# Selective scans: state feeds on GpSimd from B rows repeated by DMA, decays in PSUM, and per-direction storage for a walk by chunks

## The chip, the cores and the metric

The kernel runs on one core of one Trainium2 chip. Its time is the device time of one execution in microseconds; given are three runs and their median. The engines are TensorE (PE; its weight loads are PEld), VectorE (DVE), ScalarE (ACT), GpSimd (POOL) and SyncE (SP, which issues DMAs).

## The reference

Four layers follow one another on an input of 4 x 192 x 56 x 56 in float32: a windowed attention with a mixer, a channel gate, a strip attention with a gated feed-forward block, and a selective scan over the image in four directions. Only the last one is touched. What it computes:

```python
xn = _ln_cf(x, ln_w, ln_b)
xz = jnp.einsum('dc,bchw->bdhw', in_proj_w, xn)
xc, z = jnp.split(xz, 2, axis=1)
xc = silu(depthwise_conv3x3(xc, conv_w) + conv_b)
x_hw = xc.reshape(Bsz, D, L)
x_wh = xc.transpose(0, 1, 3, 2).reshape(Bsz, D, L)
xs = jnp.stack([x_hw, x_wh, x_hw[..., ::-1], x_wh[..., ::-1]], axis=1)
x_dbl = jnp.einsum('kcd,bkdl->bkcl', x_proj_w, xs)
dts, Bv, Cv = jnp.split(x_dbl, [R, R + N], axis=2)          # R = 12, N = 4 states
dt = jax.nn.softplus(jnp.einsum('kdr,bkrl->bkdl', dt_proj_w, dts) + dt_proj_b[None, :, :, None])
A = -jnp.exp(A_log)
# per step:  h = exp(dt*A) * h + dt * B * u;   y = sum over states of h * C
ys = _selective_scan(xs, dt, A, Bv, Cv) + Ds[None, :, :, None] * xs
# the four directions are brought back to image order and added, then
# layernorm, * silu(z), output projection, + x
```

For each of 4 images, 192 channels, 4 directions (rows, columns, and both backwards) and 4 states a linear recurrence of 3136 steps is run.

## The kernel before, in words

The program is a row of stages, each with its own tiles and semaphores and a barrier behind it. Two are touched: `scan_inputs` (L2928) and `scans` (L3553). `scan_outputs` (L3310) follows and is not touched.

**scan_inputs** takes the image in 14 steps: two pairs of images, 7 chunks of 448 pixels (8 rows of 56). The 384 channels of an image pair are laid over 128 partitions x 3. For each step it normalizes (`square`, `root`, `normal`), projects (`project`), convolves with 27 operations on VectorE (`taps`), applies Silu (`inputs`) and makes two small products (`small`, PE L3120): the 48 rows of step sizes for all directions (`pD`) and the 32 rows of B and C (`pB`). ScalarE copies the first to `f_do` (L3196), the second in bf16 to `f_bo` (L3198); VectorE takes the remainder (L3291), ScalarE rounds it (L3202), VectorE takes the next one (L3295), so that B and C are stored as three bf16 parts, 96 rows in all. SP stores them in image order (`store_small` L3024, `store_steps` L3031). The ScalarE order in a step is square, maps, halo, root, small, middle, gates, inputs (L3217 to L3235).

**scans** walks 24 sections: 2 image pairs x 3 groups of 128 channels x 4 directions, in the order `ORDER = (0, 2, 1, 3)`. A section has 7 chunks, a chunk 2 units of two states each: 168 chunks, 336 units `j`. The order of work on every engine is written out by hand; semaphores join them.
- VectorE, per unit: `scan(j)` (two TENSOR_TENSOR_SCAN, L3884, in place in `h`, start value from the unit before last), `feed(j + 1)` (L3869: step input times B, to `h`), `read(j)` (L3891: `h` times C, to `prod`).
- TensorE: `spread` (L3705) multiplies a selector with the bf16 rows of B or C so that one row appears on all 128 partitions of PSUM, two states side by side in `pB` and in `pC` (one tile each); `add` (L3722) sums the products of all states into `pY` by an identity matrix, with the skip term or what another direction left; `step` (L3695) makes the step sizes of the next section from 12 rows.
- ScalarE: `parts` and `softened` (L3781 to L3801: Relu, Abs, Exp, Ln for softplus; the odd directions are written turned, with a stride), `decay` (L3811: exp(dt*A), to four SBUF tiles `s_da`), `evacuate` (L3824), and the turned copies `column` (L3773) and `column_x` (L3779, 3136 elements at once).
- GpSimd: `step_size` (L3907, Relu part plus Ln part) and `step_input` (L3918, dt times x) of the next section, one behind each unit's scans (L3930), and the store of the result (L3922).
- SP: x, B and C rows, and the 12 step rows of a chunk (L3665), four buffers.

The step sizes `dt` and step inputs `dtu` are whole-image tiles, two each, so a section's step sizes are all made before its first unit. All sections start from step rows, B and C rows in image order; the column directions are turned on ScalarE.

L1238 and L1239, in an earlier stage, load a row of 192 numbers onto 128 and 112 partitions by a DMA that repeats the row; they are read in the rows below.

```python
                u = dtu[s % 2][:, span(c)].rearrange("p (o n) -> p o n", o=1).broadcast_to([128, 2, CH])
                v.tensor_tensor(h[j % 4][:, :, :], u, pB[:, :, 0:CH], ALU.mult).then_inc(b_used, 1)
```

Of the kernel before, what the change touches and what calls it, by code (L numbers as in the profile page):

```python
# [16 lines left out]
N = H * W  # L17
# [79 lines left out]
SR = 4  # L97
RP = 10
# [2829 lines left out]
def scan_inputs(nc, x3, kept, xc, zs, dts, bcs):  # L2928
# [4 lines left out]
    with ExitStack() as ctx:  # L2933
# [28 lines left out]
        bo = [sb(f"f_bo{i}", [64, 3, CH], BF16) for i in range(NO)]  # L2962
        pA, pI, pD, pB = pt("f_pa", 3), pt("f_pi", 3), pt("f_pd"), pt("f_pb")
# [23 lines left out]
        dts_evac = sem("f_dts_evac")  # L2987
        hi_done = sem("f_hi_done")
# [4 lines left out]
        x_stored = [sem(f"f_x_stored{i}") for i in range(NO)]  # L2993
        block = ctx.enter_context(nc.Block())
# [18 lines left out]
        def _(sp):  # L3013
# [5 lines left out]
            def store_small(s):  # L3019
                q, o = s // NCH, s % NO  # L3020
                sp.wait_ge(lo_done, s + 1)
                sp.wait_ge(mid_done, s + 1)
                for i in range(2):
                    sp.dma_start(bcs[2 * q + i, :, span(s)].rearrange("(m r) n -> r m n", m=3),  # L3024
                                 bo[o][32 * i:32 * i + 32, :, :]).then_inc(x_stored[o], 16)

            def store_steps(s):
                q, o = s // NCH, s % NO
                sp.wait_ge(dts_evac, s + 1)
                for i in range(2):  # L3030
                    sp.dma_start(dts[2 * q + i, :, span(s)], do[o][64 * i:64 * i + NK, :]).then_inc(x_stored[o], 16)  # L3031
# [36 lines left out]
        def _(pe):  # L3068
# [51 lines left out]
            def small(s):  # L3120
# [10 lines left out]
                if s:  # L3131
                    pe.wait_ge(rest_done, s)
# [20 lines left out]
        def _(a):  # L3153
# [84 lines left out]
        def _(v):  # L3238
# [314 lines left out]
def scans(nc, xc, dts, bcs, dt_wT, dt_b, a_log, ds, sel, ident, ys):  # L3553

    with ExitStack() as ctx:
        sb = lambda name, shape, dt=F32: ctx.enter_context(nc.sbuf_tensor(name, shape, dt))  # L3560
# [16 lines left out]
        dt = [sb(f"s_dt{i}", [128, N]) for i in range(2)]  # L3577
        dtu = [sb(f"s_dtu{i}", [128, N]) for i in range(2)]
# [461 lines left out]
```

## Time and profile before

| | us |
|---|---|
| median of 3 runs | 5881.08 |
| lowest, highest | 5874.78, 5885.37 |
| profiled execution, span from first to last instruction | 5874.6 |
| profiled execution, its own time | not shown apart from the span |
| busy in the span: PE, DVE, ACT, POOL | 5234.5, 4111.9, 2823.1, 805.7 |
| DMA | 398.22 MB, mean 68 GB/s |

The span is one execution on the chip as the hardware profiler saw it. Busy time is the time in which an engine had an instruction under way; records of matmuls overlap, so a busy TensorE is not one at its peak. Starts are counted from the start of the span. A row of a timeline may hold several equal instructions (x2), and then gives their time together. "idle <-" names what ended the idle time ahead of an instruction.

### The profile page before, as it was taken

Reading aid. Unit: us, or ns where it says so; the run is one execution under the profiler, and the core shown is the slowest. Engines: PE = TensorE matmul, PEld = TensorE weight load, DVE = VectorE, ACT = ScalarE, POOL = GpSimd, SP = SyncE. Lnnn points to the kernel's source line nnn. Section 1 sums busy time; section 2 is a strip of 40 time slices with the busy share of each in tenths; the row PEclk is TensorE's granted clock in tenths of the full one; section 3 lists DMA queues with packets and bytes.
Section 4 is the critical chain, followed back from the end, with each engine's and each line's share of the span. In section 5 each row is a group of like instructions: output and inputs, shape, how many; then the busy total and the mean of one; then the engine's idle time right before and its main releaser. Section 6 shows DMA issues by size and latency. Waiting matters only on the chain. (4 is left out here: it accounts for less than half of the span.)

```text
span 5874.6 us, 85825 instructions
## 1 busy us (share of the span) xinstructions
PE 5234.5 (89%) x34692; PEld 2383.9 (41%) x34692; DVE 4111.9 (70%) x4899; ACT 2823.1 (48%) x3955; POOL 805.7 (14%) x826
## 2 busy tenths in 40 slices
PE   7799999999989989968869799989778888888879
PEld 2355555555544434445534333333233333333323
DVE  3477677776621122278878499959789999999963
ACT  1144444444432223245521455526587777867844
POOL 1000000000000011122243100000033333323300
PEclk9899999999999989989989899989889999999999
DMA  6522121221032223344433000013300000000034
GB/s 214 138 39 42 22 42 23 40 43 22 15 110 70 81 77 129 111 142 142 132 119 123 29 29 29 33 47 113 99 29 29 5 28 25 16 29 5 17 113 164
DMA packets 298982, 398.22 MB, mean 68 GB/s; under 512 B 143916, under 2 KB 281316, under 8 KB 295324
## 3 DMA queue, kind: packets, MB, share of 16 engines
q1 hardware_dynamic: 271452, 302.90, 17.6%
q0 software_dynamic: 16096, 73.39, 3.7%
q10 hardware_dynamic: 11040, 16.43, 0.9%
q8 instruction: 276, 4.52, 0.3%
q14 instruction: 118, 0.97, 0.1%
HBM read 226.16 MB, written 166.49 MB: 67 GB/s over the span
## 5 line engine op out<-in xcount | busy, mean ns | idle before, releaser
L3884 DVE TENSOR_TENSOR_SCAN s_h<-s_da,s_h 128x448 f32<-128x448 f32 x672 | 729.6, 1124 | 1.5 <-ACT s_da L3811 1.4
L3731 PE MATMUL s_py<-s_prod,s_idf 128*128 128x448 f32 x1344 | 586.6, 559 | 24.5 <-ACT s_ycol L3824 23.3
L622 PE MATMUL b_pc<-b_ca,b_wdm 128*113 128x392 f32 x1152 | 486.9, 520 | 31.9 <-DVE b_wdm L837 25.8
L3811 ACT ACTIVATE s_da<-s_dt,s_al 128x448 f32<-128x448 f32 x672 | 406.1, 658 | 198.3 <-DVE s_h L3884 147.6
L765 ACT ACTIVATE b_band<-b_psel 124x784 f32<-124x784 f32 x264 | 217.7, 825 | 427.5 <-PE b_psel L690 424.4
L622 PE MATMUL b_pc<-b_cb,b_wdm 128*113 128x392 f32 x960 | 403.0, 520 | 0.0
L3869 DVE TENSOR_TENSOR s_h<-s_dtu,s_pb 128x896 f32<-128x896 f32 x336 | 354.9, 1056 | 31.7 <-POOL s_dtu L3918 23.2
L3891 DVE TENSOR_TENSOR s_prod<-s_h,s_pc 128x896 f32<-128x896 f32 x336 | 360.8, 1074 | 0.1
L3907 POOL TENSOR_TENSOR s_dt<-s_dt,s_dtu 128x448 f32<-128x448 f32 x168 | 249.3, 1484 | 782.7 <-DVE s_h L3884 427.5
L2861 DVE SCALAR_TENSOR_TENSOR j_zc<-j_zt,kept_vec,j_zc 128x896 f32<-128x896 f32 x320 | 344.9, 1144 | 6.7 <-ACT j_zt L2803 6.4
L3731 PEld LDWEIGHTS s_py<-s_prod,s_idf 128*128 128x128 f32 x1344 | 249.2, 193 | 220.0 <-issue 167.3
L1059 DVE TENSOR_SCALAR b_band<-b_psel 124x784 f32<-124x784 f32 x104 | 101.3, 974 | 236.4 <-PE b_psel L690 235.3
L1374 ACT ACTIVATE c_hid<-c_ph,c_vec 128x448 f32<-128x448 f32 x168 | 106.2, 634 | 332.1 <-PE c_ph L1333 318.4
L749 ACT ACTIVATE b_at<-b_pbt 128x448 bf16<-128x448 bf16 x336 | 164.6, 543 | 168.7 <-PE b_pbt L668 168.7
L622 PEld LDWEIGHTS b_pc<-b_ca,b_wdm 128*113 128x113 f32 x1152 | 176.0, 178 | 137.0 <-issue 86.7
L2394 PE MATMUL e_pc<-e_at,e_diag 128*128 128x448 f32 x504 | 195.4, 549 | 37.7 <-ACT e_at L2421 37.6
L3791 ACT ACTIVATE s_dt<-s_pd,s_db 128x448 f32<-128x448 f32 x168 | 144.1, 858 | 141.7 <-PE s_pd L3702 141.7
L707 PE MATMUL b_po<-b_band,b_vt 124*32 124x112 f32 x5376 | 203.1, 275 | 1.2 <-ACT b_band L765 1.2
L3278 DVE SCALAR_TENSOR_TENSOR f_cv<-f_ct,kept_vec,f_cv 128x448 f32<-128x448 f32 x336 | 202.3, 672 | 0.0
L707 PEld LDWEIGHTS b_po<-b_band,b_vt 124*32 124x32 f32 x5376 | 153.2, 111 | 103.9 <-issue 103.2
L1267 POOL MEMSET kept_f_wt<- 128x192 f32 x1 | 0.3, 258 | 1416.1 <-POOLq L143 1416.1
L3702 PE MATMUL s_pd<-s_dtt,s_wd 12*128 12x448 f32 (+1 forms) x448 | 174.1, 589 | 20.6 <-DVE s_skip L3858 11.6
(726 smaller groups left out, 11252.0 us busy)
## 6 DMA issues: line engine op xcount, KB each, us to landing
b_qk<-mid_qkvp SPq DMA_DIRECT2D x96, 240.2 KB
d_vt<-mid_vd SPq DMA_DIRECT2D x200, 96.0 KB
d_qs<-mid_qd SPq DMA_DIRECT2D x20, 744.0 KB, 5.3
d_ks<-mid_kd SPq DMA_DIRECT2D x20, 744.0 KB, 7.7
b_v<-mid_qkvp SPq DMA_DIRECT2D x6, 1922.0 KB
mid_pout<-d_out POOLq DMA_DIRECT2D x20, 558.0 KB, 4.4
mid_qkvp<-a_out SPq DMA_DIRECT2D x42, 248.0 KB, 2.2
mid_qkvp<-a_out ACTq DMA_DIRECT2D x42, 248.0 KB, 2.1
```

Source lines behind the costliest of these rows:

```text
L622: mm = pe.matmul(pc[n % 2][0:113, 0:392], wdm[:, slot, p, 0:113], src, start=(w == STARTS[a]), stop=(w + 1 == STARTS[a + 1]))
L707: mm = pe.matmul(pO[32 * g:32 * g + 32, 112 * s:112 * s + 112], vt[:, 14 * hf + 4 * s + g + d, 32 * (h % 4):32 * (h % 4) + 32], band[hf][: ...
L765: a.activation(band[hf][:, 2 * dp:2 * dp + 2, c0:c0 + 2, :, :, :, :].rearrange("p d c t r a i -> p d (c t r a i)"), selection(h, x)[0:124, ...
L2394: mm = pe.matmul(pc[k % 2][t][:, 0:CH], diag[:, t, i, :], at[k % 4][:, t, dy:dy + 8, dx:dx + W], start=(i == 0), stop=(i == 8))
L2861: v.scalar_tensor_tensor(dst, src, gw[:, t, k:k + 1], dst, ALU.mult, ALU.add).then_inc(tap_done, 1)
L3278: v.scalar_tensor_tensor(dst, tap, cw[:, t, k:k + 1], dst, ALU.mult, ALU.add).then_inc(tap_done, 1)
L3731: mm = pe.matmul(y, idf[:, :], prod[j % 3][:, e, :], start=(pr == 0 and e == 0), stop=False)
L3811: last = a.activation(da[j % 4][:, e, :], dt[s % 2][:, span(c)], ACT.Exp, scale=al[:, u, n:n + 1])
L3869: v.tensor_tensor(h[j % 4][:, :, :], u, pB[:, :, 0:CH], ALU.mult).then_inc(b_used, 1)
L3884: v.tensor_tensor_scan(x, along(da[j % 4][:, e, :]), x, before_, ALU.mult, ALU.add).then_inc(scanned, 1)
L3891: v.tensor_tensor(prod[j % 3][:, :, :], h[j % 4][:, :, :], pC[:, :, 0:CH], ALU.mult).then_inc(c_used, 1)
L3907: p.tensor_tensor(put(dt[s % 2]), put(dt[s % 2]), put(dtu[s % 2]), ALU.add).then_inc(dt_ready, 1)
```

## The change

In `scans`:
- The feeds go from VectorE to GpSimd. B comes as float32 rows from DRAM: a DMA per chunk (two where a channel group spans two images) repeats the four rows of a direction over the partitions, into three tiles `s_bt`. TensorE spreads C alone; the B and C tiles in SBUF become one C tile, both images on its 96 partitions.
- The decays are written to PSUM: three tiles of one state each take the place of four SBUF tiles of two.
- Step rows, B rows and step sizes are stored in each direction's own order, so nothing in `parts` and `softened` is turned any more. `dt`, `dtu`, the Relu part and the Abs part are rings of chunks (4, 4, 6 and 3 pairs), and each chunk's step sizes are made six chunks ahead. Exp and Ln run on two chunks at once. x is turned by chunks.
- `h` has 6 tiles. VectorE's order per unit is scan(j), read(j - 1). The store of the result goes from GpSimd's queue to SP's.

In `scan_inputs`: ScalarE makes three more copies in each step (B and C in float32, and the step rows and the B and C rows once turned, into whole-image tiles); the remainder is taken from the float32 copy in SBUF, and SP stores B in float32 and C in three bf16 parts.

```diff
 scan_inputs
+        bf = [sb(f"f_bf{i}", [64, CH]) for i in range(NO)]
+        dcol = sb("f_dcol", [128, N])
+        bcol = sb("f_bcol", [64, N])
...
 store_small(s)
+                sp.wait_ge(b_evac, s + 1)
                 for i in range(2):
-                    sp.dma_start(bcs[2 * q + i, :, span(s)].rearrange("(m r) n -> r m n", m=3),
-                                 bo[o][32 * i:32 * i + 32, :, :]).then_inc(x_stored[o], 16)
+                    sp.dma_start(cs[2 * q + i, :, span(s)].rearrange("(m r) n -> r m n", m=3),
+                                 bo[o][32 * i + 16:32 * i + 32, :, :]).then_inc(x_stored[o], 16)
+                    sp.dma_start(brs[2 * q + i, s % NCH, 0:8, :], bf[o][32 * i:32 * i + 8, :]).then_inc(x_stored[o], 16)
+                if s % NCH == NCH - 1:
+                    for i in range(2):
+                        sp.dma_start(brs[2 * q + i, :, 8:16, :].rearrange("c r n -> r c n"),
+                                     bcol[32 * i + 8:32 * i + 16, :].rearrange("r (c n) -> r c n", c=NCH)).then_inc(col_stored, 16)
...
 small(s), ScalarE
+                if s == NCH:
+                    a.wait_ge(col_stored, 64)
-                a.activation(do[o][:, :], pD[:, 0, 0:CH], ACT.Copy).then_inc(dts_evac, 1)
+                a.activation(do[o][:, :], pD[:, 0, 0:CH], ACT.Copy)
+                a.activation(turned(dcol[:, :], s % NCH), img(pD[:, 0, 0:CH]), ACT.Copy).then_inc(dts_evac, 1)
                 a.wait_ge(bc_done, s + 1)
                 a.activation(bo[o][:, 0, :], pB[0:64, 0, 0:CH], ACT.Copy).then_inc(hi_done, 1)
+                a.activation(bf[o][:, :], pB[0:64, 0, 0:CH], ACT.Copy)
+                a.activation(turned(bcol[:, :], s % NCH), img(pB[0:64, 0, 0:CH]), ACT.Copy).then_inc(b_evac, 1)
...
 remainder(s)
+                v.wait_ge(b_evac, s + 1)
-                v.tensor_tensor(rest[:, :], pB[0:64, 0, 0:CH], bo[s % NO][:, 0, :], ALU.subtract).then_inc(rest_done, 1)
+                v.tensor_tensor(rest[:, :], bf[s % NO][:, :], bo[s % NO][:, 0, :], ALU.subtract).then_inc(rest_done, 1)
...
 scans
+        DR, UR, RR, ER, HR, BR = 4, 4, 6, 3, 6, 3
+        AHEAD = 6
+        bt = [sb(f"s_bt{i}", [128, NST, CH]) for i in range(BR)]
-        da = [sb(f"s_da{i}", [128, 2, CH]) for i in range(4)]
+        da = [pt(f"s_da{i}") for i in range(3)]
...
 SP
+            def load_b(t):
+                s, q, u, k, c = place(t)
+                if t >= BR:
+                    sp.wait_ge(fed, 2 * (t - BR + 1))
+                r = NST * (s % KD)
+                for i, d0, p0, m in PIECES[u]:
+                    rows = brs[2 * q + i, c, r:r + NST, :].rearrange("r n -> (r n)")
+                    sp.dma_start(bt[t % BR][p0:p0 + m, :, :].rearrange("p r n -> p (r n)"), rows.partition_broadcast(m)).then_inc(b_loaded[t % BR], 16)
...
+            load_step(0)
+            load_step(1)
+            load_x(0)
+            load_b(0)
+            load_step(2)
+            load_step(3)
+            load_c(0)
+            load_b(1)
+            load_b(2)
...
+            for t in range(NTS):
+                s, i = divmod(t, NCH)
+                if t + AHEAD + 2 < NTS:
+                    load_step(t + AHEAD + 2)
+                if t + BR < NTS:
+                    load_b(t + BR)
+                if s % KD == 1 and i == 0 and s // KD + 1 < NV:
+                    load_x(s // KD + 1)
+                if s % NSEC == NSEC - 2 and i == 0 and s // NSEC + 1 < NP2:
+                    load_c(s // NSEC + 1)
+                if s and s % KD == 0 and i == 3:
+                    store(s // KD - 1)
...
 TensorE
             for j in range(NJ):
+                t, pr = divmod(j, 2)
+                if pr == 0 and t + AHEAD < NTS:
+                    step(t + AHEAD)
                 if j + 1 < NJ:
+                    spread(j + 1)
+                add(j)
...
 ScalarE
+            def decay(m):
+                t, n = divmod(m, NST)
+                s, q, u, k, c = place(t)
+                if m >= 3:
+                    a.wait_ge(scanned, m - 2)
+                a.wait_ge(dt_ready, t + 1)
+                n += NST * k
+                a.activation(da[m % 3][:, 0, 0:CH], dt[t % DR][:, :], ACT.Exp, scale=al[:, u, n:n + 1]).then_inc(decay_ready, 1)
...
 VectorE
             for j in range(NJ):
-                if j == 0:
-                    feed(0)
                 scan(j)
-                if j + 1 < NJ:
-                    feed(j + 1)
-                read(j)
+                if j:
+                    read(j - 1)
+            read(NJ - 1)
...
 GpSimd
+            def feed(j):
+                t, pr = divmod(j, 2)
+                p.wait_ge(dtu_ready, t + 1)
+                p.wait_ge(b_loaded[t % BR], b_count(t))
+                if j >= HR:
+                    p.wait_ge(c_used, j - HR + 1)
+                    p.wait_ge(scanned, 2 * (j - HR + 3))
+                u = dtu[t % UR][:, :].rearrange("p (o n) -> p o n", o=1).broadcast_to([128, 2, CH])
+                p.tensor_tensor(h[j % HR][:, :, :], u, bt[t % BR][:, 2 * pr:2 * pr + 2, :], ALU.mult).then_inc(fed, 1)
...
             for j in range(NJ):
+                t, pr = divmod(j, 2)
+                if pr == 0 and t + 2 < NTS:
+                    step_size(t + 2)
+                if pr == 1 and t + 2 < NTS:
+                    step_input(t + 2)
+                if j + 2 < NJ:
+                    feed(j + 2)
```

## Rows read from the trace of the kernel before

**Rows 1.** Stretches: length, busy of PE, PEld, DVE, ACT, POOL, clock, DMA share, GB/s

```profile
3946.00:4256.00 310.00, 278.83 (x964) 92.62 (x962) 255.39 (x424) 195.34 (x248) 0.00 (x0) 0.96 0.31 102
4278.00:5660.00 1382.00, 1169.37 (x3903) 446.29 (x3904) 1368.74 (x1344) 1027.61 (x1517) 437.63 (x334) 0.98 0.05 18
```

**Rows 2.** Groups of instructions by line and shape, 4256 to 5665 us

```profile
L3884 DVE TENSOR_TENSOR_SCAN s_h<-s_da,s_h 128x448 f32<-128x448 f32 x672 | 729.6, 1124 | 1.5 <-ACT s_da L3811 1.4
...
L3731 PE MATMUL s_py<-s_prod,s_idf 128*128 128x448 f32 x1344 | 586.6, 559 | 24.5 <-ACT s_ycol L3824 23.3 <-DVE s_prod L3891 1.3
...
L3811 ACT ACTIVATE s_da<-s_dt,s_al 128x448 f32<-128x448 f32 x672 | 406.1, 658 | 198.3 <-DVE s_h L3884 147.6 <-POOL s_dt L3907 50.7
...
L3891 DVE TENSOR_TENSOR s_prod<-s_h,s_pc 128x896 f32<-128x896 f32 x336 | 360.8, 1074 | 0.1
...
L3869 DVE TENSOR_TENSOR s_h<-s_dtu,s_pb 128x896 f32<-128x896 f32 x336 | 354.9, 1056 | 31.7 <-POOL s_dtu L3918 23.2 <-PE s_pb L3719 8.6
...
L3907 POOL TENSOR_TENSOR s_dt<-s_dt,s_dtu 128x448 f32<-128x448 f32 x168 | 249.3, 1484 | 782.7 <-DVE s_h L3884 427.5 <-ACT s_dtu L3801 355.2
...
L3719 PE MATMUL s_pb<-s_bct,s_sel 96*128 96x448 bf16 x224 | 64.6, 371 | 35.0 <-DVE s_h L3869 33.8
...
L3779 ACT ACTIVATE s_xcol<-s_xt 128x3136 f32<-128x3136 f32 x6 | 36.5, 6090 | 0.0
...
L3719 PE MATMUL s_pb<-s_bct,s_sel 96*64 96x448 bf16 x224 | 31.8, 364 | 12.3 <-DVE s_h L3869 11.8
```

**Rows 3.** Timeline of VectorE, 4500 to 4514 us

```profile
4500.67 2.17 DVE L3884 TENSOR_TENSOR_SCAN s_h<-s_da,s_h 128x448 f32<-128x448 f32 x2
4502.77 1.05 DVE L3869 TENSOR_TENSOR s_h<-s_dtu,s_pb 128x896 f32<-128x896 f32 x1
4503.75 1.07 DVE L3891 TENSOR_TENSOR s_prod<-s_h,s_pc 128x896 f32<-128x896 f32 x1
4504.75 2.17 DVE L3884 TENSOR_TENSOR_SCAN s_h<-s_da,s_h 128x448 f32<-128x448 f32 x2
```

**Rows 4.** Timeline of GpSimd, 4500 to 4514 and at the start of the scans

```profile
4277.88 10.06 POOL L3918 TENSOR_TENSOR s_dtu<-s_dt,s_xt 128x448 f32<-128x448 f32 x7
...
4502.92 1.13 POOL L3907 TENSOR_TENSOR s_dt<-s_dt,s_dtu 128x448 f32<-128x448 f32 x1 [2.94 <-DVE s_h L3884]
4507.00 1.14 POOL L3918 TENSOR_TENSOR s_dtu<-s_dt,s_xt 128x448 f32<-128x448 f32 x1 [2.94 <-DVE s_h L3884]
```

**Rows 5.** Timeline of VectorE at the start and at the end of the scans

```profile
4279.04 1.09 DVE L3869 TENSOR_TENSOR s_h<-s_dtu,s_pb 128x896 f32<-128x896 f32 x1 [23.18 <-POOL s_dtu L3918]
4280.24 3.79 DVE L3884 TENSOR_TENSOR_SCAN s_h<-s_da,s_h 128x448 f32<-128x448 f32 x2
4283.95 1.05 DVE L3869 TENSOR_TENSOR s_h<-s_dtu,s_pb 128x896 f32<-128x896 f32 x1
...
5656.94 1.09 DVE L3891 TENSOR_TENSOR s_prod<-s_h,s_pc 128x896 f32<-128x896 f32 x1
```

**Rows 6.** Groups of GpSimd instructions by line and shape, whole span

```profile
L2351 POOL TENSOR_TENSOR e_rows<-e_pin 128x672 f32<-128x672 f32 x14 | 21.2, 1514 | 69.0 <-DMA e_pin<-mid_pout 68.2 <-POOL e_t L2372 0.7
...
L2361 POOL TENSOR_TENSOR e_s<-e_rows 128x21 f32<-128x21 f32 x14 | 3.5, 251 | 1.1
```

**Rows 7.** Groups of VectorE instructions by line and shape, whole span

```profile
L2903 DVE TENSOR_TENSOR j_z<-j_zc,j_z 128x896 f32<-128x896 f32 x13 | 14.1, 1085 | 0.0
```

**Rows 8.** DMA rate in 40 slices of 0.25 us, 1732 to 1742 us

```profile
GB/s 373 344 409 387 416 387 416 394 401 409 409 382 336 371 384 299 218 284 313 332 350 406 378 396 406 372 270 92 52 61 209 357 433 424 393 406 393 406 393 406
```

**Rows 9.** DMA rate in 40 slices of 0.4 us, 4254 to 4270 us

```profile
GB/s 160 85 103 99 354 63 220 157 470 408 439 408 345 428 502 361 329 314 235 235 267 172 267 267 298 204 258 208 126 65 45 54 22 18 0 0 0 0 0 0
```

**Rows 10.** Timelines of ScalarE and VectorE, 4090 to 4112 us (scan_inputs)

```profile
4093.20 0.53 ACT L3196 ACTIVATE f_do<-f_pd 128x448 f32<-128x448 f32 x1
4097.23 0.58 ACT L3202 ACTIVATE f_bo<-f_rest 64x448 bf16<-64x448 f32 x1 [2.65 <-DVE f_rest L3291]
...
4096.59 0.61 DVE L3291 TENSOR_TENSOR f_rest<-f_pb,f_bo 64x448 f32<-64x448 f32 x1
```

More of the change, by code:

```diff
@@ L3690, in _ @@
+            store(NV - 1)
+            for i in range(2):
+                sp.wait_ge(stored[i], 16 * NV // 2)
         @block.tensor
@@ L3720, in spread @@
-                mm.then_inc(done, 1)
+                        col = KD * NST * i + row
+                        mm = pe.matmul(pC[p0:p0 + m, e, 0:CH], selt[:, col:col + 1].broadcast_to([G, m]), src[:, span(c)], start=True, stop=True)
+                mm.then_inc(c_spread, 1)
             def add(j):
-                s, c, pr = place(j)
-                q, u, k = section(s)
-                t, v = j // 2, s // KD
+                t, pr = divmod(j, 2)
+                s, q, u, k, c = place(t)
+                v = s // KD
@@ L3778, in column_x @@
                     a.wait_ge(dtu_ready, NCH * KD * v)
-                a.activation(turned(xcol[:, :]), img(xt[v % 2][:, :]), ACT.Copy).then_inc(xcol_ready, 1)
-            def parts(s, c):
-                q, u, k = section(s)
-                n = NCH * s + c
-                if s >= 2:
-                    a.wait_ge(dtu_ready, NCH * (s - 1))
-                    a.wait_ge(decay_ready, UNITS * (s - 1))
-                    a.wait_ge(b_used, UNITS * (s - 1))
-                a.wait_ge(step_done, n + 1)
-                put = lambda t: turned(t[:, :])[:, 8 * c:8 * c + 8, :] if k % 2 else img(t[:, span(c)])
-                a.activation(put(dt[s % 2]), img(pD[n % 2][:, 0, 0:CH]), ACT.Relu, bias=db[:, u, k:k + 1])
-                a.activation(put(dtu[s % 2]), img(pD[n % 2][:, 0, 0:CH]), ACT.Abs, bias=db[:, u, k:k + 1]).then_inc(step_evac, 1)
@@ L3794, in softened, with parts @@
-            def softened(s, c):
-                k = ORDER[s % KD]
-                e = turned(dtu[s % 2][:, :])[:, 8 * c:8 * c + 8, :] if k % 2 else dtu[s % 2][:, span(c)]
-                n = NCH * s + c + 1
-                a.wait_ge(step_evac, n)
+                a.activation(img(xcol[:, span(c)]), turned(xt[v % 2][:, :])[:, 8 * c:8 * c + 8, :], ACT.Copy).then_inc(xcol_ready, 1)
+            def parts(t):
+                s, q, u, k, c = place(t)
+                if t >= RR:
+                    a.wait_ge(dt_ready, t - RR + 1)
+                a.wait_ge(step_done, t + 1)
+                a.activation(raw[t % RR][:, :], pD[:, 0, 0:CH], ACT.Relu, bias=db[:, u, k:k + 1])
+                a.activation(soft[t // 2 % ER][:, t % 2, :], pD[:, 0, 0:CH], ACT.Abs, bias=db[:, u, k:k + 1]).then_inc(step_evac, 1)
@@ L3824, in evacuate @@
                 a.activation(put, img(got) if k >= 2 else got, ACT.Copy).then_inc(y_evac, 1)
-            for c in range(NCH):
-                parts(0, c)
-                softened(0, c)
+            parts(0)
+            parts(1)
+            shrunk(0)
+            softened(0)
+            parts(2)
+            parts(3)
             a.wait_ge(a_ready, 2)
@@ L3939, in _, with step_size @@
-            store(3 * NP2 - 1)
-            for i in range(2):
-                p.wait_ge(stored[i], 16 * 3 * NP2 // 2)
+            def step_size(t):
+                p.wait_ge(log_taken, t // 2 + 1)
+                if t >= DR:
+                    p.wait_ge(decay_ready, NST * (t - DR + 1))
+                    p.wait_ge(dtu_ready, t - DR + 1)
+                p.tensor_tensor(dt[t % DR][:, :], raw[t % RR][:, :], soft[t // 2 % ER][:, t % 2, :], ALU.add).then_inc(dt_ready, 1)
+            def step_input(t):
+                s, q, u, k, c = place(t)
+                v = s // KD
+                p.wait_ge(dt_ready, t + 1)
+                if k == 1:
+                    p.wait_ge(xcol_ready, NCH * v + c + 1)
+                elif k == 3:
+                    p.wait_ge(xcol_ready, NCH * (v + 1))
+                else:
+                    p.wait_ge(x_loaded[v % 2], 16 * (v // 2 + 1))
+                if t >= UR:
+                    p.wait_ge(fed, 2 * (t - UR + 1))
+                x = xcol if k % 2 else xt[v % 2]
+                p.tensor_tensor(dtu[t % UR][:, :], dt[t % DR][:, :], x[:, span(c)], ALU.mult).then_inc(dtu_ready, 1)
@@ L3950, in network @@
+    return np.kron(np.eye(2), np.tile(np.eye(n), (3, 1))).astype(mybir.dt.np(BF16))
 def network(nc, a, s, out):
```

294 lines of the change are left out of this document (127 added, 167 removed).

## Prediction, made before the changed kernel was built or run

> **What bounds the kernel now.** I first read the table of busy times by stretch, for the two stages that the diff touches [rows 1]. In the scans, 4278 to 5660 us, VectorE is busy for 1368.7 of 1382.0 us, TensorE for 1169.4, ScalarE for 1027.6 and GpSimd for 437.6, with a DMA share of 0.05. So VectorE bounds this stage, a fourth of the whole span. Next come the groups by line [rows 2]: VectorE runs 672 scans, 336 feeds (L3869) and 336 reads (L3891), nothing else. Then the timeline of a steady stretch [rows 3]: two scans start at 4500.67, the feed at 4502.77, the read at 4503.75, the next scans at 4504.75. A unit (two states of one chunk) thus costs 2.10 + 0.98 + 1.00 = 4.08 us, without a gap, and a chunk, two units, 8.16 us. GpSimd's work starts at 4502.92, 0.08 us behind the scans' end (L3928 makes it wait for them), and lasts 1.13 us [rows 4].
>
> The whole walk, first feed to last read, is 4279.0 to 5658.0 [rows 5], 1379.0 us for 168 chunks (8.21 each).
>
> **The feeds.** 336 feeds leave VectorE. A unit is left with 2.10 + 1.00 = 3.10 us, a chunk with 6.20, the walk with 168 x 6.20 = 1042 us, if GpSimd delivers. On GpSimd a chunk now has one L3907 (1.13 us, always unit stride; its mean was 1484 ns because half of them were turned [rows 2]), one L3918 (1.14) and two feeds of 128x896. No such feed is in the trace. GpSimd's additions of two tensors took 251 ns for 21 elements and 1514 for 672 [rows 6], 1.94 ns an element; from 21 elements to the 448 of rows 4 it is (1.13 - 0.25)/427 = 2.06. So a feed costs between 1.13 + 448 x 0.00194 = 2.00 us and twice a 448, 2.26. I take 1.13 + 448 x 0.00206 = 2.05, since the 448 rows are the nearest in kind. Between instructions there is at most the 0.08 us seen behind a scan, and nothing where waits are met early; a feed has four waits. I take 0.04 each, ends 0 and 0.08. Sum: 1.13 + 1.14 + 2 x 2.05 + 4 x 0.04 = 6.53 us a chunk (ends 6.27 and 7.12). That is over 6.20: **GpSimd becomes the bound**, VectorE waits 0.33 us a chunk, and the walk is 168 x 6.53 = 1097.0. Less the 2.3 us of the first step size and input, which lie ahead of the first feed, plus the 4.3 of the last scans and reads behind the last feed, it is 1099.0, against 1379.0: **-280.0** (ends -324 and -181).
>
> The GPSIMD Engine Reference of the Trainium skill (3.1 and 4.1) speaks against such a move: elementwise work belongs on VectorE, GpSimd is about 2x slower with two inputs, 4497 ns for 2048 elements. By that page a feed would be estimated at 896/2048 x 4497 = 1967 ns and a chunk at 6.37 us, 27 us less than my sum.
>
> **The decays in PSUM.** The time of a scan from PSUM is not in the trace. A product with one operand in PSUM took 1056 ns (L3869, 896 elements [rows 2]), one of the same size with both in SBUF 1085 (L2903 [rows 7]), so PSUM does not cost VectorE more. I price a scan at the same 2.10 us a pair; it would have to rise by 0.16 us a pair before VectorE passes GpSimd. What the move is worth is read at the stage's start. The seven first step inputs run on GpSimd from 4277.88, back to back, in 10.06 us, 2.1 more than 7 x 1.14 [rows 4]; the first scan pair beside them takes 3.79 us instead of 2.17, while the next feed, with one operand in PSUM, takes its usual 1.05 [rows 5]. So a scan with both inputs in SBUF and GpSimd hold each other up, and a VectorE instruction with one input in PSUM does not. With the decays in PSUM all VectorE work of the stage is of the second kind: I put contention at zero, with the rival below for the case that it is not. The page SBUF — State Buffer of the Trainium skill ("Who interferes with whom") states this as a rule: at most one SBUF input, no contention; by it rival 3 has no time at all.
>
> **ScalarE.** Even with all its old work, 1027.6/168 = 6.12 us a chunk, it stays under 6.53. Its Relu, Abs, Exp and Ln lose their turned halves, and the last two are done for pairs of chunks, so it falls further. Four decays of 658 ns stay [rows 2]; three buffers let it run one to two scans ahead, and with that slack the largest single piece (a turned x chunk, 6090/7 = 870 ns) doesn't reach VectorE: 0.
>
> **TensorE.** The B spreads go: for the untransposed half they are 64.6 + 31.8/2 us (the 64-wide ones run in twos) [rows 2], for both halves about 161. There remain (1169.4 - 161)/168 = 6.0 us a chunk of records that overlap their followers, under 6.53: 0, though PE is the next one behind. Behind each read stand a C spread, the additions (559 ns a record) and at every other unit a step; the new order puts the spread first, so VectorE's next read, two scans later, finds it. Cover gone, PE would take over at 6.0, so it can cost nothing unless GpSimd is faster than I say. The granted clock was 0.98 (2.4 GHz level) at 85% busy; I see no reason for a fall.
>
> **B rows by DMA.** SP's queue gets one or two DMAs a chunk, 128 x 1792 x 4 B = 917 KB, 154 MB in all, in front of or behind the x loads, the stores and the step rows of the same queue. At 6.53 us a chunk that is 140 GB/s, in a stage that moved 18. The nearest row is the stretch with the repeated rows of L1238 and L1239: 0.25 us slices of 344 to 416 GB/s for ordinary loads, 270 at their start, then 92, 52, 61 and 209, back to 357 [rows 8]. Those four slices average 103, the five with the 270 are 137; the packets there are 768 B, against 7 KB now. So bounds are 103 and 400 GB/s, 8.9 and 2.3 us a chunk; I take 2.3 to 3.5, since these rows are long. Three buffers give two chunks, 13 us, from the feed that frees one to its next use; x and y (1568 KB, 4 us at 400) fit beside. Cost 0, cover GpSimd.
>
> **Start and stores.** The stage now waits for one chunk's chain, not seven. Before, the loads ran from 4254 at 0.4 us a slice and were over by 4268 [rows 9]; x, one B tile and the first steps, 1.57 + 0.92 + 0.2 = 2.7 MB, are through by 4264 if the same slices are added up, and landing and a step input (1.14) follow: first feed at 4266.5, not 4279.0: **-12.5** (0 to -15). GpSimd's store goes to SP, which waits for the evacuation of a chunk three back while B loads queue behind it; they have two chunks' cover: 0.
>
> **The stage before** (scan_inputs, 3946 to 4256). ScalarE gets three more copies in each of 14 steps: one plain (0.53 us, L3196 [rows 10]) and two turned; a turned 448 takes 870 ns inside one long copy [rows 2], and alone it pays its own start, so I take 1.05 to 1.1. In the trace ScalarE starts its small copies at 4093.20, VectorE the remainder at 4096.59, the middle copy at 4097.23 [rows 10]. Now the small copies end at 4093.2 + 0.5 + 1.05 + 0.5 + 0.5 + 1.1 = 4096.9: 0.3 us late, 14 times 4 us. Behind the last step 2.6 us of copies and four more DMA issues and landings lie open: 5. Sum **+9** (0 to +20).
>
> **Sum.** 5874.6 - 280.0 - 12.5 + 9 = 5591.1 us of span. The profiled execution's own time is not shown beside its span; the median of three runs is 6.5 over it, which I add: **5598 us**, 283 under 5881.
>
> **Rivals.**
> 1. VectorE stays the bound: a feed takes under 1.9 us on GpSimd. Then 6.20 a chunk, 55 less: 5543. For it: the slope of 1.94 and early waits; against it: 448 elements never took under 1.13. Chance 0.08.
> 2. The B rows bound: every descriptor reads the same 7 KB. At 131 GB/s a chunk takes 7.0 us, the walk 79 more: 5677; at the lowest 103 it is 8.9, and 5990. For it: the slices at 52 to 92; against it: the first of these rows passed at 270. Chance 0.10, most of it under 5850.
> 3. Slower than before: GpSimd still locks out the scans, because they write or take their start value in SBUF. Then 4.2 us of scans and 6.4 of GpSimd stand one behind the other, 10.6 us a chunk, 168 x (10.6 - 6.53) = 684 more: 6282. It decides from where 40% of the scan time ((8.21 - 6.53)/4.2) is so held. For it: 3.79 against 2.17; against it: the unhindered feed beside GpSimd. Chance 0.05.
> 4. Waits between the chunk rings (steps, soft pairs, decays) leave 0.3 to 1 us a chunk: 5650 to 5770. The trace of before has longer rings. Chance 0.09.
>
> The forecast has 0.68.
>
> **How the numbers follow.** Its own ends are 5598 - 44 = 5554 and 5598 + 99 + 11 = 5708. With rival 1 below and the nearer parts of 2 and 4 above, 5540 to 5725 leaves out two in ten. A measurement can tell 0.2%, 12 us. Slower: rival 3, and 0.02 of rival 2, 0.07. Same: 0.01. Faster: 0.92.
>
> **What would show it.** GpSimd over 95% busy in the walk with feeds of 2.0 to 2.1 us; VectorE waiting for GpSimd some 50 us in total; scan slots still 2.10 a pair; a walk of about 1100 us; DMA at 140 GB/s without GpSimd waiting for B tiles; the first feed near 4276 (9 us later start); scan_inputs 9 us longer. Wrong is: scans of 1.5 us or more beside feeds, GpSimd waiting on a DMA, or feeds over 2.3 us.

## The result and the profile after

| | us |
|---|---|
| after, median of 4 runs | 5559.86 (5545.01 to 5563.93) |
| before, beside it, median of 4 runs | 5881.15 (5874.78 to 5885.37) |
| ratio | 0.9446, 95% interval 0.9432 to 0.9461 |
| profiled execution after | span 5560.1, own time 5562.28 |

The kernel is 5.5% faster, 38 us under the forecast and inside its range. The page of the changed kernel, its costliest groups in the scans and the two B transfers (last two lines: KB each, us from issue to landing):

```profile
PE 5052.6 (91%) x33796; PEld 2334.1 (42%) x33796; DVE 3792.1 (68%) x4563; ACT 2672.0 (48%) x3851; POOL 1419.3 (26%) x1156
...
L3926 DVE TENSOR_TENSOR_SCAN s_h<-s_da,s_h 128x448 f32<-128x448 f32 x672 | 730.2, 1128 | 26.1 <-ACT s_da L3853 22.6
L3973 POOL TENSOR_TENSOR s_h<-s_dtu,s_bt 128x896 f32<-128x896 f32 x336 | 698.7, 2080 | 0.1
...
L3853 ACT ACTIVATE s_da<-s_dt,s_al 128x448 f32<-128x448 f32 x672 | 401.9, 637 | 13.0 <-DVE s_h L3926 12.9
...
L3933 DVE TENSOR_TENSOR s_prod<-s_h,s_pc 128x896 f32<-128x896 f32 x336 | 356.8, 1062 | 1.4 <-issue 0.7
...
L3948 POOL TENSOR_TENSOR s_dt<-s_raw,s_soft 128x448 f32<-128x448 f32 x168 | 189.7, 1129 | 348.5 <-ACT s_soft L3844 348.5
...
s_bt<-mid_brs SPq DMA_DIRECT2D x112, 896.0 KB, 4.4
s_bt<-mid_brs SPq DMA_DIRECT2D x112, 448.0 KB, 5.8
```

The scans cost what they cost before, 1128 ns against 1124, and so do the reads [rows 2]; the feeds have gone to GpSimd, at 2080 ns. Of GpSimd's 348.5 us of idle time 345.5 lie ahead of its first instruction in the stage; behind it there are 3. The busy times by stretch, to be held against [rows 1] (length, then PE, PEld, DVE, ACT, POOL, clock, DMA share, GB/s):

```profile
3946.00:4256.00 310.00, 284.71 (x980) 95.06 (x980) 256.04 (x420) 228.44 (x292) 0.00 (x0) 0.97 0.30 98
4280.00:5345.00 1065.00, 988.50 (x3016) 395.02 (x3017) 1047.10 (x1008) 858.19 (x1392) 1053.47 (x670) 0.99 0.54 166
```

In the scans GpSimd is busy for 98.9% and VectorE for 98.3%: two engines at their limit at once, and TensorE at 93% behind them. A steady stretch shows which of the two leads. First GpSimd's timeline, then VectorE's:

```profile
4698.56 2.08 POOL L3973 TENSOR_TENSOR s_h<-s_dtu,s_bt 128x896 f32<-128x896 f32 x1
4700.62 1.12 POOL L3963 TENSOR_TENSOR s_dtu<-s_dt,s_xt 128x448 f32<-128x448 f32 x1
4701.71 2.08 POOL L3973 TENSOR_TENSOR s_h<-s_dtu,s_bt 128x896 f32<-128x896 f32 x1
4703.76 1.14 POOL L3948 TENSOR_TENSOR s_dt<-s_raw,s_soft 128x448 f32<-128x448 f32 x1
4704.86 2.08 POOL L3973 TENSOR_TENSOR s_h<-s_dtu,s_bt 128x896 f32<-128x896 f32 x1
```

```profile
4700.69 2.19 DVE L3926 TENSOR_TENSOR_SCAN s_h<-s_da,s_h 128x448 f32<-128x448 f32 x2
4702.79 1.06 DVE L3933 TENSOR_TENSOR s_prod<-s_h,s_pc 128x896 f32<-128x896 f32 x1
4703.82 2.19 DVE L3926 TENSOR_TENSOR_SCAN s_h<-s_da,s_h 128x448 f32<-128x448 f32 x2
4705.93 1.06 DVE L3933 TENSOR_TENSOR s_prod<-s_h,s_pc 128x896 f32<-128x896 f32 x1
4706.98 2.19 DVE L3926 TENSOR_TENSOR_SCAN s_h<-s_da,s_h 128x448 f32<-128x448 f32 x2
```

From start to start GpSimd's four instructions are 2.06, 1.09, 2.05 and 1.10 us: a chunk takes 6.30, without a gap. A record is longer than its slot (2.08 for 2.05), because the next instruction's record begins before it ends. VectorE's units are 3.13 and 3.16 in turn, 6.29 a chunk, GpSimd's pace, and each scan pair starts 0.03 to 0.05 us behind the end of a feed (4700.64, 4703.79, 4706.94): GpSimd leads. VectorE by itself is faster. At the start of the walk, where feeds lie ready ahead of it, its unit is 2.11 + 0.97 = 3.08:

```profile
4296.27 2.19 DVE L3926 TENSOR_TENSOR_SCAN s_h<-s_da,s_h 128x448 f32<-128x448 f32 x2
4298.38 1.06 DVE L3933 TENSOR_TENSOR s_prod<-s_h,s_pc 128x896 f32<-128x896 f32 x1
4299.35 1.15 DVE L3926 TENSOR_TENSOR_SCAN s_h<-s_da,s_h 128x448 f32<-128x448 f32 x1
```

The last feeds and the last read:

```profile
5330.27 6.18 POOL L3973 TENSOR_TENSOR s_h<-s_dtu,s_bt 128x896 f32<-128x896 f32 x3
```

```profile
5342.43 1.09 DVE L3933 TENSOR_TENSOR s_prod<-s_h,s_pc 128x896 f32<-128x896 f32 x1 [0.70 <-PE s_pc L3771]
```

The first feed starts at 4279.66, so the walk, first feed to last read, is 5343.5 - 4279.7 = 1063.8 us, against 1379.0: -315.1. What lies ahead of the scans varies from one execution to the next: in the changed kernel and those below, the stage's first table load starts anywhere from 4249.4 to 4266.2, the first feed from 4263.4 to 4282.4. The walk doesn't hold that variation, and is the measure in all that follows. Two executions of the changed kernel gave walks of 1063.8 and 1061.1 us, so a difference of 3 us between single walks says nothing.

The start of the scans on ScalarE and GpSimd:

```profile
4263.38 1.28 ACT L3811 ACT_TABLE_LOAD   x1 [8.43 <-PEq L144]
...
4270.88 0.63 ACT L3833 ACTIVATE s_raw<-s_pd,s_db 128x448 f32<-128x448 f32 x1 [2.90 <-PE s_pd L3753]
...
4276.22 0.95 ACT L3844 ACTIVATE s_soft<-s_soft 128x896 f32<-128x896 f32 x1
```

```profile
4277.25 1.12 POOL L3948 TENSOR_TENSOR s_dt<-s_raw,s_soft 128x448 f32<-128x448 f32 x1 [345.54 <-ACT s_soft L3844]
4278.45 1.13 POOL L3963 TENSOR_TENSOR s_dtu<-s_dt,s_xt 128x448 f32<-128x448 f32 x1
4279.66 2.07 POOL L3973 TENSOR_TENSOR s_h<-s_dtu,s_bt 128x896 f32<-128x896 f32 x1
```

From the stage's table load to the first feed it is 16.3 us; before, from 4250.30 to 4279.04 [rows 5], it was 28.7.

The whole difference of the two profiled executions, 5874.6 - 5560.1 = 314.5 us, is made up so: walk -315.1, start -12.5, end of scan_inputs +5.6, and +7.4 that arise between 2154 and 3045 us, in stages that the change doesn't touch. What follows the walk takes 216.6 us in both.

### The profile page after: what moved, and what is told of

Read it like the earlier page. It is cut to its first block and busy times, and to the rows that moved or that the text cites. A ratio compares the mean times of both kernels' runs of the same rounds, so it can differ in the third digit from the quotient of the medians.

```text
span 5560.1 us, 84741 instructions
## 1 busy us (share of the span) xinstructions
PE 5052.6 (91%) x33796; PEld 2334.1 (42%) x33796; DVE 3792.1 (68%) x4563; ACT 2672.0 (48%) x3851; POOL 1419.3 (26%) x1156
## 5 line engine op out<-in xcount | busy, mean ns | idle before, releaser
L3926 DVE TENSOR_TENSOR_SCAN s_h<-s_da,s_h 128x448 f32<-128x448 f32 x672 | 730.2, 1128 | 26.1 <-ACT s_da L3853 22.6
L3973 POOL TENSOR_TENSOR s_h<-s_dtu,s_bt 128x896 f32<-128x896 f32 x336 | 698.7, 2080 | 0.1
L3783 PE MATMUL s_py<-s_prod,s_idf 128*128 128x448 f32 x1344 | 573.9, 549 | 0.0
L3948 POOL TENSOR_TENSOR s_dt<-s_raw,s_soft 128x448 f32<-128x448 f32 x168 | 189.7, 1129 | 348.5 <-ACT s_soft L3844 348.5
L3833 ACT ACTIVATE s_raw<-s_pd,s_db 128x448 f32<-128x448 f32 x168 | 106.4, 633 | 195.0 <-PE s_pd L3753 195.0
```

The source lines that it names most:

```text
L3783: mm = pe.matmul(y, idf[:, :], prod[j % 3][:, e, :], start=(pr == 0 and e == 0), stop=False)
L3926: v.tensor_tensor_scan(x, along(da[m % 3][:, 0, 0:CH]), x, before_, ALU.mult, ALU.add).then_inc(scanned, 1)
L3948: p.tensor_tensor(dt[t % DR][:, :], raw[t % RR][:, :], soft[t // 2 % ER][:, t % 2, :], ALU.add).then_inc(dt_ready, 1)
L3973: p.tensor_tensor(h[j % HR][:, :, :], u, bt[t % BR][:, 2 * pr:2 * pr + 2, :], ALU.mult).then_inc(fed, 1)
```

## The experiments

Each kernel is the changed one with the edit shown. The first four have one profiled run each, beside a run of before at 5884.93 us.

**Decays back in SBUF.** Do the PSUM decays keep GpSimd and the scans apart?

```diff
-        da = [pt(f"s_da{i}") for i in range(3)]
+        da = [sb(f"s_da{i}", [128, 1, CH]) for i in range(3)]
```

> The changed kernel with its three decay tiles in SBUF instead of PSUM, nothing else. Reference point: in the changed kernel the walk (first feed to last read) is 1064 us, 6.3 us a chunk. Theory (a scan with both inputs in SBUF and GpSimd's instructions hold each other up): GpSimd is never idle, so scans (4.2 us a chunk) and GpSimd's work (6.3) stand largely one behind the other: 8.5 to 10.5 us a chunk, walk 1430 to 1770 us, single scans up to 3 us. Rival (the decays' place does not matter, the unhindered first feed in the trace of before was luck): 6.3 us a chunk, walk within 10 us of 1064.

Measured: 6079.4 us, slower than before the change; the walk is 1587.1 us, as the theory had it. VectorE's timeline, then GpSimd's:

```profile
4701.68 3.81 DVE L3926 TENSOR_TENSOR_SCAN s_h<-s_da,s_h 128x448 f32<-128x448 f32 x2
4705.41 1.06 DVE L3933 TENSOR_TENSOR s_prod<-s_h,s_pc 128x896 f32<-128x896 f32 x1
4706.39 3.80 DVE L3926 TENSOR_TENSOR_SCAN s_h<-s_da,s_h 128x448 f32<-128x448 f32 x2
```

```profile
4702.61 1.92 POOL L3948 TENSOR_TENSOR s_dt<-s_raw,s_soft 128x448 f32<-128x448 f32 x1
4704.50 2.86 POOL L3973 TENSOR_TENSOR s_h<-s_dtu,s_bt 128x896 f32<-128x896 f32 x1
4707.33 1.92 POOL L3963 TENSOR_TENSOR s_dtu<-s_dt,s_xcol 128x448 f32<-128x448 f32 x1
```

A scan pair takes 3.73 us from start to start, not 2.10, and GpSimd's instructions are 0.8 us longer each; the read, with one operand in PSUM, keeps its 1.06. A unit takes 4.71 us. It isn't that scans from SBUF are slow by themselves: before the change their decays lay in SBUF too, and a scan took 1124 ns, with GpSimd mostly waiting. Only the decays changed place, and the walk is half a millisecond longer. The whole gain hangs on this one line.

**Feeds back on VectorE**, from the same SBUF B tiles, decays in PSUM. What does the rest of the change give without the move?

```diff
+            def feed(j):
...
+                v.tensor_tensor(h[j % HR][:, :, :], u, bt[t % BR][:, 2 * pr:2 * pr + 2, :], ALU.mult).then_inc(fed, 1)
             for j in range(NJ):
+                if j == 0:
+                    feed(0)
                 scan(j)
+                if j + 1 < NJ:
+                    feed(j + 1)
                 if j:
                     read(j - 1)
```

> The changed kernel with the feeds back on VectorE, B still from the tiles loaded by DMA, decays still in PSUM, rings and storage as changed. Theory (only the move of the feeds shortened the walk, the rest of the change is worth nothing there by itself): VectorE has 2.10 + 1.00 + 0.98 = 4.08 us a unit, walk 1371 us, plus what GpSimd's two instructions a chunk cost the feeds, which now have both inputs in SBUF: 1371 to 1500. Rival (the rings by chunk and the unit stride shorten the walk too): under 1320.

Measured: 5896.8 us, walk 1406.3. The groups of VectorE in the scans:

```profile
L3926 DVE TENSOR_TENSOR_SCAN s_h<-s_da,s_h 128x448 f32<-128x448 f32 x672 | 727.0, 1121 | 8.4 <-ACT s_da L3853 8.4
L3943 DVE TENSOR_TENSOR s_h<-s_dtu,s_bt 128x896 f32<-128x896 f32 x336 | 386.2, 1150 | 10.7 <-POOL s_dtu L3977 10.7
```

So without the move B rows by DMA, PSUM decays and chunk rings bring nothing to the walk; it is even 27 us longer than before. The feed group shows where: 386.2 us against 354.9 with B in PSUM [rows 2], 31 more. Most feeds take 1.05 or 1.07, and those beside a GpSimd addition up to 2.00. That is the hold of the experiment above again, now on a product whose operands are both in SBUF. The page SBUF — State Buffer of the Trainium skill ("Who interferes with whom") has it as a rule that a VectorE instruction with two inputs in SBUF contends with a GpSimd instruction that reads SBUF. Both runs agree, with scans of 1940 ns (median) beside GpSimd and feeds of up to 2.00 us. The walk's 315 us come with the feeds' place, given the PSUM decays. What the rest of the change does bring is the earlier start of the stage, 16.1 us from table load to first feed here too.

**A shorter read on VectorE.** Is VectorE a bound too? Left out: 64 of 448 columns of each product with C (the product tiles are set to zero once at the start).

```diff
-                v.tensor_tensor(prod[j % 3][:, :, :], h[j % HR][:, :, :], pC[:, :, 0:CH], ALU.mult).then_inc(c_used, 1)
+                v.tensor_tensor(prod[j % 3][:, :, 0:384], h[j % HR][:, :, 0:384], pC[:, :, 0:384], ALU.mult).then_inc(c_used, 1)
```

> The changed kernel with reads over 384 of 448 columns: the last 64 columns of each chunk's products are left out. VectorE has 0.27 us a chunk less, GpSimd the same. Theory (GpSimd bounds the walk at 6.29 us a chunk, VectorE with 6.20 is just behind): the walk stays at 1064 us within 5, and VectorE's idle time grows by 45 us. Rival (VectorE bounds): walk 45 us shorter, 1019.

Measured: 5553.45 us, walk 1061 us, what the unedited kernel has when it is run again (below). 336 reads are 0.13 us shorter, 44 us in all, and none of it is seen: GpSimd leads. VectorE's idle time ahead of its scans goes from 26.1 to 58.6 us, 32 of the 45 that were expected; the rest shows in no row.

**A shorter addition on GpSimd.** Left out: 224 of 448 columns of each step-size addition (those columns are set to a constant once at the start).

```diff
-                p.tensor_tensor(dt[t % DR][:, :], raw[t % RR][:, :], soft[t // 2 % ER][:, t % 2, :], ALU.add).then_inc(dt_ready, 1)
+                p.tensor_tensor(dt[t % DR][:, 0:224], raw[t % RR][:, 0:224], soft[t // 2 % ER][:, t % 2, 0:224], ALU.add).then_inc(dt_ready, 1)
```

> The changed kernel with the step size (Relu part plus Ln part) made by GpSimd for 224 of 448 columns, a constant in the others: half of that addition is left out. GpSimd has about 0.5 us a chunk less (5.8), VectorE the same 6.20. Theory (GpSimd bounds, VectorE is 0.1 behind): the walk gets 10 to 16 us shorter, 1048 to 1054, with VectorE busy over 99% and GpSimd idle 0.4 us a chunk. Rival (VectorE bounds already): walk 1064 within 3. Rival (both wait on something else, TensorE or the B loads): walk 1064 within 3 and VectorE still idle.

Measured: 5528.96 us, walk 1041.8. GpSimd was spared 0.47 us a chunk, 79 us, and the walk fell by 22. Over 1010 us of it the busy times are these (columns as in the stretches above):

```profile
4290.00:5300.00 1010.00, 963.47 (x2967) 385.24 (x2965) 1009.88 (x990) 839.70 (x1364) 959.46 (x658) 1.00 0.56 172
```

VectorE is idle for 0.1 us, and GpSimd is down to 95%: the bound has changed hands. The unit is 3.08 throughout, VectorE's own time as seen at the start of the changed kernel's walk, not the 3.10 that I had counted with: its read slot is 0.98, and the 1.03 and 1.05 in the changed kernel's steady stretch had 0.05 to 0.07 us of waiting in them that no row names. Hence a walk 6 us under the low end of what I expected.

**Both at once**, run last of all, beside a run of before at 5881.19 us. Its edit is the two above together.

> Left out of the computation: each read takes 384 of its 448 columns and each step-size addition 224 of 448. Alone, the shorter read left the walk of the scans at 1060.9 us (1063.8 in the changed kernel) and the shorter addition brought it to 1041.8. Theory (the two engines stand within a few per cent of each other, each with its own sum a chunk): GpSimd's chunk is 2 x 2.05 + 1.09 + some 0.6 = 5.8 us, VectorE's is 2 x (2.10 + 0.86) = 5.92 us, so the walk comes to 168 x 5.92 or a little more, 995 to 1012 us, with VectorE busy for over 98% of it. Rival (what is left of the stage is bound by something else, TensorE's queue of 5.6 to 6.0 us a chunk or the decays on ScalarE): it stays at 1025 to 1042 us.

Measured: 5507.03 us, walk 1011 us, 6.02 a chunk, at the upper end of the theory's range. Against the 1063.8 the read alone gave 3 us, the addition 22, both 53 (against the 1061.1 of the second execution: 0, 19 and 50). The stretch:

```profile
4290.00:5290.00 1000.00, 978.86 (x3009) 393.25 (x3008) 988.69 (x1006) 851.09 (x1383) 967.28 (x664) 0.99 0.56 175
```

VectorE is at 98.9% with units of 2.95 us in steady stretches. TensorE's records, which overlap, cover 97.9%; whether it would be the third bound wasn't tried.

The next four ran on one chip, beside 9 runs of before with the median 5882.81: the first with one run, the others with 4, 5 and 4.

**B rows loaded once.** Left out: the B tiles of all but the first three chunks, so the feeds multiply stale B rows. Are the loads hidden?

```diff
-            return 16 * sum(len(PIECES[place(i)[2]]) for i in range(t % BR, t + 1, BR))
+            return 16 * len(PIECES[place(t % BR)[2]])
...
-                if t + BR < NTS:
-                    load_b(t + BR)
```

> The changed kernel with the B tiles loaded for the first three chunks only and used for all 168: 151 MB of loads are left out (and with them the right B). Theory (the B loads are hidden behind GpSimd): walk 1064 us within 4, DMA share in the walk down from 0.54 to under 0.1. Rival (they hold the feeds or the scans up, by late tiles or by sharing SBUF): walk over 10 us shorter.

Measured: 5557.86 us, walk 1062.3 at 24 GB/s instead of 166. A difference of 1.5 us for some 150 MB (1065 us at 142 GB/s): they are hidden. In the changed kernel each load comes as a burst. The DMA rate in 40 slices of 1 us from 4700 us:

```profile
GB/s 380 36 0 0 93 337 423 108 0 0 0 237 437 287 0 0 0 115 409 375 63 0 0 108 387 375 90 18 0 50 344 366 371 301 131 0 151 409 375 35
```

Most slices that a load fills stand at 337 to 437 GB/s, and between two loads the queues are mostly idle. Over the same 40 us in slices of 0.25 us, as in [rows 8], low slices are still there near the start of a load, but one or two at a time (86 GB/s at 4705.0, 29 at 4717.75, 57 and 143 at 4736.5), where [rows 8] has four in a row.

**The changed kernel again**, as a control, with no edit.

> The changed kernel once more, as the control for the next two on the same chip: 5545 to 5565 us, walk 1064 us.

Measured: 5553.54 us (5544.73 to 5561.93), ratio 0.9441 (0.9428 to 0.9453), walk 1061.1.

**Softplus as ln(1 + exp(x)).** GpSimd's addition of the two parts goes, as ScalarE takes Exp straight from PSUM and Ln writes the step size; `dt` becomes a ring of three pairs.

```diff
-                a.activation(raw[t % RR][:, :], pD[:, 0, 0:CH], ACT.Relu, bias=db[:, u, k:k + 1])
-                a.activation(soft[t // 2 % ER][:, t % 2, :], pD[:, 0, 0:CH], ACT.Abs, bias=db[:, u, k:k + 1]).then_inc(step_evac, 1)
+                a.activation(soft[t // 2 % ER][:, t % 2, :], pD[:, 0, 0:CH], ACT.Exp, bias=db[:, u, k:k + 1]).then_inc(step_evac, 1)
...
-                a.activation(e, e, ACT.Exp, scale=-1.0).then_inc(exp_taken, 1)
...
-                a.activation(e, e, ACT.Ln, bias=1.0).then_inc(log_taken, 1)
+                a.activation(dt[g % ER][:, :, :], soft[g % ER][:, :, :], ACT.Ln, bias=1.0).then_inc(dt_ready, 2)
...
-                p.tensor_tensor(dt[t % DR][:, :], raw[t % RR][:, :], soft[t // 2 % ER][:, t % 2, :], ALU.add).then_inc(dt_ready, 1)
```

> The changed kernel with softplus as ln(1 + exp(x)) on ScalarE, written straight to the step sizes, in place of Relu, Abs, Exp, Ln there and an addition on GpSimd. GpSimd has 2 x 2.05 + 1.09 = 5.2 us a chunk left, ScalarE one instruction less. Theory (GpSimd bounds at 6.29, VectorE at 6.16 to 6.20 is next, TensorE at 5.6 behind it): walk 1040 to 1046 us, the kernel 15 to 25 us under the control, VectorE busy over 99% of the walk. Rival (TensorE or the loads come next before VectorE): walk over 1055 us, and VectorE idle.

Measured: 5528.61 us (5525.60 to 5543.34), ratio 0.9403 (0.9390 to 0.9416), walk 1044.7. The stretch:

```profile
4290.00:5300.00 1010.00, 963.04 (x2967) 385.45 (x2966) 1009.14 (x989) 694.40 (x1122) 857.79 (x491) 1.00 0.56 171
```

VectorE is the bound, at 99.9%, with GpSimd at 85% and ScalarE at 69%; walk and kernel (24.9 us under the control) are as the theory had them. The form has no guard for large x, where exp(x) overflows; the Relu and Abs form has one.

**The same with another start**: eight step-row buffers, six step rows issued ahead of the first B tile, the first two chunks' Ln taken one by one, and three decays ahead of the third chunk.

```diff
-SR = 4
+SR = 8
...
+            for t in range(2, 6):
+                load_step(t)
...
-            parts(0)
-            parts(1)
-            shrunk(0)
-            softened(0)
+            for t in range(2):
+                parts(t)
+                a.wait_ge(step_evac, t + 1)
+                a.activation(dt[0][:, t, :], soft[0][:, t, :], ACT.Ln, bias=1.0).then_inc(dt_ready, 1)
+                if t == 0:
+                    a.wait_ge(a_ready, 2)
+                    decay(0)
+                    decay(1)
+                    decay(2)
```

> The kernel of e_direct with another beginning of the scans: eight step-row buffers, six of them loaded ahead of the first B tile, softplus of the first two chunks one by one, and three decays made ahead of the later step sizes. In the changed kernel VectorE's first scan starts at 4284 and its second unit only at 4293, 14 us behind GpSimd's first feed. Theory (VectorE bounds now, so its own late start counts in full): 8 to 14 us under e_direct. Rival (the lag is made up behind the rings of six units, as GpSimd runs ahead): within 3 us of e_direct.

Measured: 5527.06 us (5521.24 to 5529.88), ratio 0.9394 (0.9382 to 0.9407), walk 1034.0, 10.7 shorter than without the new start. VectorE's start, in the changed kernel and then in this one:

```profile
4284.19 2.07 DVE L3926 TENSOR_TENSOR_SCAN s_h<-s_da,s_h 128x448 f32<-128x448 f32 x2 [15.28 <-ACT s_da L3853]
4293.31 2.07 DVE L3926 TENSOR_TENSOR_SCAN s_h<-s_da,s_h 128x448 f32<-128x448 f32 x2 [7.05 <-ACT s_da L3853]
```

```profile
4280.13 4.10 DVE L3921 TENSOR_TENSOR_SCAN s_h<-s_da,s_h 128x448 f32<-128x448 f32 x4 [12.62 <-POOL s_h L3961]
```

The 7 us wait ahead of the second unit is gone. But part of the walk's gain is a later first feed: it waits for its B tile, behind the extra step rows, until 16.0 us after the stage's table load, against 14.0 in the kernel without the new start. Counted from the table load to the last read the stage takes 1050.0 against 1058.7 us, 8.7 less. In the kernel's time, of which the expectation spoke, the two medians are only 1.5 us apart, with overlapping intervals. In the two profiled executions the stages ahead of the scans took 12.6 us longer with the new start (table load at 4262.1 against 4249.4), in which the edit changes nothing; that covers the stage's gain there. The gain stands in one profiled execution each, and whether it reaches the total isn't settled.

## Why the prediction was right, and where it was 38 us high

**The feeds.** Right in mechanism: GpSimd took the bound and VectorE stood just behind. The term was mis-sized, "6.53 us a chunk" against 6.30. Its feed of 2.05 was right, as the slot (its record is 2.08). The two additions have slots of 1.09 and 1.10, not 1.13 and 1.14, which is 0.08: I used the length of lone records as if it were their slot. And "0.04 each" for the waits between the four instructions, 0.16 a chunk, was nothing: the timeline has no gap. From the first feed's start to the last feed's end it is 1056.8 us against the 1094.7 of the working, and from there to the last read's end 7.1 instead of 4.3: the last three feeds have no addition between them and follow at 2.06 us each, faster than VectorE's units of 3.08, so the last scans start 2.1 us behind the last feed's end, and the last read waits another 0.7 for its C. Together the walk is 35.2 us under the forecast. By the figure of the Trainium skill (GPSIMD Engine Reference, 3.1) the estimates were 1967 ns a feed and 6.37 us a chunk. That was nearer for the chunk, but by luck: its feed is too short (2.05 us as a slot, 2080 ns as a record), and this made up for the same additions and waits that I had too long.

**VectorE's wait.** "0.33 us a chunk, some 50 us in total" was wrong with it. The rows name 26.1 us ahead of the scans, nearly all of it at the start (15.3 + 7.1) and for ScalarE's decays, not for GpSimd. The waiting for GpSimd is the difference between units of 3.08 at the start and 3.13 and 3.16 later, 0.13 us a chunk. The two engines were 2% apart rather than 5, so little was missing for rival 1 (VectorE stays the bound). With GpSimd eased it is what happens: VectorE alone bounds the versions without the addition, at 6.16 us a chunk in its slots, where the rival had 6.20.

**The decays in PSUM.** Right: pairs kept their 2.10 beside a GpSimd that is never idle, and without PSUM the hold is there. Rival 3 had the hold come from the scans' write and start value in SBUF. The changed kernel has both there, and its scans aren't held; it is the second input in SBUF that does it. The rival's price for a held walk, 10.6 us a chunk, is not far from that of the run with the decays in SBUF, 1587.1/168 = 9.4: each side was held for part of the other's instruction, not for all.

**ScalarE and TensorE at zero.** Right: 858 and 989 us of 1065, with no wait for them in a steady row. The 22.6 us that VectorE waits for ScalarE's first decays lie at the start, while GpSimd goes on with its feeds. TensorE's records were put at 6.0 us a chunk and cover 989/1065 of 6.30, 5.85.

**B rows.** Right: hidden, by the experiment. The mean is 166 GB/s: 917 KB in 6.30 us are 146, where I had 140 for a longer chunk, and the other transfers of the stage come on top. Rival 2 falls (its far end, at 8.9 us a chunk, adds up to 5996 and not to 5990). Low slices come with these loads too, but too few to matter; what makes them wasn't tried.

**Start.** -12.5 forecast, -12.5 measured (28.74 to 16.28), but not by the wait that I had worked out, the loads' landing with a step input behind it. The first step size waits for ScalarE (345.54 <-ACT s_soft), and step size and step input lie between that and the first feed. The loads would have allowed a start about 2.3 us sooner: without the addition the feed waits for its B tile and starts 14.0 us behind the table load, not 16.3. That the number fits to 0.1 us is luck.

**scan_inputs.** +9 forecast, +5.6 measured. The tail, from the last normalization to the next stage's table load, went from 53.8 to 59.5 us, +5.6 where 5 was put. The "0.3 us late, 14 times" didn't come: the step takes 20.63 us in both kernels, though ScalarE is busy for 33 us more in the stretch (228.4 against 195.3 [rows 1]). These are the new ones:

```profile
4101.07 1.01 ACT L3219 ACTIVATE f_dcol<-f_pd 128x448 f32<-128x448 f32 x1
...
4102.34 0.51 ACT L3222 ACTIVATE f_bf<-f_pb 64x448 f32<-64x448 f32 x1
4102.76 0.99 ACT L3223 ACTIVATE f_bcol<-f_pb 64x448 f32<-64x448 f32 x1
```

**The sum.** Of the 38.1 us between 5598 and 5559.86, the walk is 35.2 and scan_inputs 3.4. The 6.5 added for the median over the span were 6.7 too many, because this kernel's median is 0.2 under its profiled span. The other way go the 7.4 us of earlier stages, in which nothing was changed. That gives 37.9. The total's error is thus nearly the walk's; the rest cancels by chance.

## What to carry to other kernels

When half of a bound engine's work moves to GpSimd, look first at where the operands of the stayed work lie: the walk came out 315 us shorter than before with the decays in PSUM, and 208 longer with them in SBUF. Price back-to-back work by slots, start to start, not by the length of a lone record, and put nothing between instructions whose waits are met early: here that would have given 6.3 us a chunk instead of 6.53. Then ask what stands within a few per cent: here two engines were balanced, and taking 79 us from one bought some 20 until the other was eased too.

## What the runs showed of the hardware that was not expected

- With both inputs of the scans in SBUF the hold was mutual and partial: a scan went from 1128 to 1933 ns in the mean (1119 to 2898), a feed on GpSimd from 2080 to 2855. Strictly one behind the other, 4.2 us of scans and 6.3 of GpSimd would make 10.5 us a chunk; 9.4 were seen. A scan whose first input is in PSUM wasn't held, though its second input, its start value and its result are in SBUF.
- The granted clock in the scans was 0.99 with TensorE busy for 93% of the time, and 0.98 at 85% [rows 1]. With the feeds back on VectorE it was 0.91 at 80%, and with the decays in SBUF 0.89 at 72%; 1.00 is the 2.4 GHz level, so these are means over spells at that one and at 1.2 GHz. It cost nothing there, since TensorE bound neither.
- One and the same read has records of different length in different kernels: slots of 0.98 us and records of 1.15 where VectorE never waits (the version without the addition, at 4700 us), and slots of 1.03 with records of 1.06 in the changed kernel. Why wasn't looked into. A record's length isn't the price of the instruction.
